# Projecting the next pass's queries, keys and values during the later stages of a two-layer decoder

## Time and profile before

| | |
|---|---|
| Median of 3 runs | 1396.28 us (1387.24 to 1396.66) |
| Profiled execution | 1388.13 us, span 1386.4 us |
| Granted TensorE clock, mean | 0.963 |
| PE busy | 1161.0 us, 84% |
| DVE, ACT, POOL busy | 54%, 53%, 27% |
| DMA | 14 GB/s over the span |

### The profile page before, as it was taken

How to read it: one execution, slowest core, us unless ns; L and a number is a source line. 1 busy time by engine, 2 the same in 40 slices (tenths; PEclk the granted TensorE clock), 3 DMA queues, 4 the chain that set the end, 5 groups by cost and what they waited for, 6 DMA issues and landing times.

```text
span 1386.4 us, 19831 instructions
## 1 busy us (share of the span) xinstructions
PE 1161.0 (84%) x6458; PEld 770.1 (56%) x6458; DVE 750.3 (54%) x1815; ACT 732.8 (53%) x1866; POOL 380.4 (27%) x881
## 2 busy tenths in 40 slices
PE   6897876999899976799889977699989997779955
PEld 2454544775555644676455554477555564467643
DVE  1563375655464368546545437655545436855644
ACT  1555345575465355557456534556645635555833
POOL 1232301542034310153213430154203332016420
PEclk9998998999999999899999999899999999989978
DMA  9101300000000000000000000000000000000000
GB/s 248 63 1 54 93 1 1 1 1 1 1 0 17 1 23 1 3 0 1 1 1 16 1 23 1 2 1 1 1 1 0 17 1 1 1 1 1 1 0 16
DMA packets 27895, 20.77 MB, mean 15 GB/s; under 512 B 14412, under 2 KB 27148, under 8 KB 27660
## 3 DMA queue, kind: packets, MB, share of 16 engines
q1 hardware_dynamic: 27196, 17.83, 5.0%
q10 hardware_dynamic: 592, 1.59, 0.3%
HBM read 17.32 MB, written 2.10 MB: 14 GB/s over the span
## 4 chain that ended last, share of the span: by engine, by line
PE 64%; DVE 15%; ACT 10%; issue 7%; POOL 3%; DMA 1%; ACTq 0%; SPq 0%; POOLq 0%; DVEq 0%
PE PS L495 8%; PE PS L559 7%; PE PS L841 7%; PE PS L482 5%; PE PS L572 5%; PE PS L547 4%; PE PS L586 4%; PE PS L617 4%; PE PS L602 4%; PE PS L815 3%; PE PS L706 2%; PE PS L692 2%; PE PS L853 2%; ACT work L1316 1%; DVE work L1591 1%
## 5 line engine op out<-in xcount | busy, mean ns | idle before, releaser
L1849 POOL TENSOR_TENSOR rstd<-var,minus_half 128x2 f32<-128x2 f32 x80 | 56.4, 705 | 522.3 <-DVE nmean L1409 522.3
L1138 ACT ACTIVATE work<-PS,nmax 128x256 f32<-128x256 f32 x256 | 117.9, 472 | 99.5 <-DVE nmax L1461 99.5
L1844 POOL TENSOR_TENSOR pool_pause<-minus_half 128x1 f32<-128x1 f32 x96 | 18.6, 194 | 440.3 <-DVE inv L1468 359.0
L1316 ACT ACTIVATE work<-PS,nmax 120x256 f32<-120x256 f32 x256 | 118.4, 483 | 24.7 <-DVE nmax L1726 24.5
L841 PE MATMUL PS<-work 128*120 128x256 f32 x512 | 119.7, 384 | 3.9 <-ACT work L1101 3.9
L1461 DVE TENSOR_REDUCE nmax<-PS 128x2 f32<-128x512 f32 x128 | 82.2, 684 | 68.7 <-PE PS L572 68.2
L1863 POOL TENSOR_SCALAR work<-work,inv 128x256 f32<-128x256 f32 x256 | 118.1, 483 | 0.0
L1726 DVE TENSOR_REDUCE nmax<-PS 120x2 f32<-120x512 f32 x128 | 86.3, 686 | 53.3 <-PE PS L841 48.6
L841 PEld LDWEIGHTS PS<-work 128*120 128x120 f32 x512 | 90.8, 183 | 29.8 <-issue 12.8
L1903 POOL TENSOR_SCALAR work<-work,head_mask 128x120 f32<-128x120 f32 x256 | 107.3, 447 | 0.0
L1109 ACT ACTIVATE x_room<-res,nshift,rstd 128x256 f32<-128x256 f32 x96 | 52.3, 592 | 101.9 <-POOL nshift L1851 101.9
(11 more groups left out here) (258 smaller groups left out, 2439.9 us busy)
## 6 DMA issues: line engine op xcount, KB each, us to landing
xa<-in_x_dram SPq DMA_DIRECT2D x4, 512.0 KB, 3.7
out_dram<-x_room SPq DMA_DIRECT2D x4, 512.0 KB, 3.7
rows<-in_rows_dram ACTq DMA_DIRECT2D x1, 1536.0 KB, 8.5
late<-in_L_attn_W_dram SPq DMA_DIRECT2D x2, 768.0 KB, 7.6
wv<-in_L_attn_kernel_dram SPq DMA_DIRECT2D x2, 512.0 KB, 8.9
wq<-in_L_attn_kernel_dram SPq DMA_DIRECT2D x2, 512.0 KB, 9.5
wk<-in_L_attn_kernel_dram SPq DMA_DIRECT2D x2, 512.0 KB, 7.7
wo<-in_L_attn_WO_dram SPq DMA_DIRECT2D x2, 512.0 KB, 7.7
```

Source lines behind the costliest of these rows:

```text
L1138: op = act.activation(e0[:, u % 2, st, hh, :], bank(2 + hh)[:, st * S:(st + 1) * S], ACT.Exp, bias=nmax0[:, u % 2, hh, st:st + 1], accum_o ...
L1316: op = act.activation(e1[:, par, r, kv, :], bank(4 + n % 4)[0:M, kv * S:(kv + 1) * S], ACT.Exp, bias=nmax1[:, par, r, kv:kv + 1], accum_ou ...
```

## The change

All 24 projections of a pass (8 half value tiles, 8 query tiles, 8 key tiles) are made before its attention begins. For pass 0 they stand at the start (`project_first`). For passes 1 to 3 they are spread over the pass before:

- `turn_input` at units 10 and 11 of the self-attention loop, from a second load of x into its own place (`x_t`, `load_x_to_turn`), copied by DVE (`keep_input`).
- In the cross-attention of layer 0 the eight value projections: two ahead of the first turn of the normed x, two behind the first query projection, four in the loop, each ahead of a weighing.
- In the feed-forward queries 0 to 3 (0 ahead of the turns of the quantized x, 1 to 3 in the tile loop), at the head of layer 1 queries 4 to 7.
- At the end of layer 1's cross-attention keys 0 to 5; in coupling rounds 0 and 1 keys 6 and 7.

Their copies out of PSUM: values and queries on ACT, keys on ACT (even) and DVE (odd). Each copy stands in its engine's queue at a fixed place, shown below. q0 and k0 now hold all eight head pairs, o0t lies over q0 (so the output projection waits for its own copies only and q0 is overwritten as it is used up), the scratch areas are laid out anew, and the PSUM banks of all later stages are moved so that bank 7, and at times 5 and 6, are free for the projections; `weigh_x` has one bank where it had two, the quantized turns one where they had two.

In attention the scores run one unit ahead, in banks 0/1 and 2/3 in turns: `scores0(u+1)` and `max0(u+1)` in the place of u. The loops over passes are written out (`for` in place of `Fori`) on all engines, SP's queue loads x and the context one pass earlier, and the DMA scratch size is set to 2048. In the attention loop nothing else on DVE or POOL changes its order.

The diff, cut to its core (the first part is PSUM and layout, then SP, PE, ACT, DVE):

```diff
+        SCORE_X = (2, 0)
+        TOKEN_X = (3, 6)
+        ATTEND = (4, 5, 3, 6)
+        SCORE_1 = (3, 4, 5, 6)
+        MLP_OUT = (2, 1)
+        QUERY_1 = (2, 0)
+        HIDDEN = (2, 6)
+        VALUE_FILL = (7, 6, 7, 6, 7, 7, 7, 7)
+        QUERY_FILL = (7, 7, 7, 7, 7, 5, 7, 5)
+        KEY_FILL = (7, 5, 7, 5, 7, 5, 7, 5)
...
-        turned_x = view(x3_room, 0, P, [KD, N])
-        work = sb("work", [P, 14016])
-        q0 = view(work, 12288, P, [2, N])
-        k0 = sb("k0", [P, 2, NB, S])
+        x_t = view(x3_room, 0, P, [T, D])
+        turned_x = sb("turned_x", [P, KD, N])
+        V, Q, K, E, R = 0, 4096, 8192, 12288, 16384
+        work = sb("work", [P, R + 2240])
+        v0 = view(work, V, P, [T, H * DH0])
+        q0 = view(work, Q, P, [J, N])
+        k0 = view(work, K, P, [J, NB, S])
+        e0 = view(work, E, P, [2, TS, 2, S])
+        e0t = view(work, E + 2048, P, [2, 2, TS, S])
-        o0t = view(work, 8192, P, [J, N])
+        o0t = q0
...
+        def load_x_to_turn(sp, it):
+            if not first_pass(it):
+                sp.wait_ge(turned["xa"].sem, turned["xa"].at(it - 1, NB))
+            if not (isinstance(it, int) and it < 2):
+                sp.wait_ge(o1_kept.sem, o1_kept.at(it - 2, GX))
+            sp.dma_start(x_t[:, :, :], x[it * NB:(it + 1) * NB].rearrange("b (t p) d -> p (b t) d", p=P)).then_inc(xt_in.sem, 16)
...
+            load_x_to_turn(sp, 1)
+            load_ctx(sp, 1)
...
+            load_x(sp, 1)
+            for it in range(1, NI - 1):
+                load_x_to_turn(sp, it + 1)
                 store(sp, it - 1)
+                load_ctx(sp, it + 1)
+                load_x(sp, it + 1)
...
+            def values0(it, n):
+                t, h = n // 2, n % 2
+                if n == 0:
+                    pe.wait_ge(kept["xa"].sem, kept["xa"].at(it, NB))
+                elif n > 1:
+                    pe.wait_ge(v0_kept.sem, v0_kept.at(it, n - 1 if n < 5 else n))
...
+            def queries0(it, j):
+                if j == 0:
+                    pe.wait_ge(v0_kept.sem, v0_kept.at(it, 2 * T))
+                elif j == 5:
+                    pe.wait_ge(silu_done.sem, silu_done.at(it - 1, T))
+                else:
+                    pe.wait_ge(q0_kept.sem, q0_kept.at(it, j if j < 5 else j - 1))
+                for k in range(KD):
+                    mm = pe.matmul(bank(QUERY_FILL[j]), wq0[:, k, j * P:(j + 1) * P], turned_x[:, k, :],
+                                   start=(k == 0), stop=(k == KD - 1))
+                mm.then_inc(q0_done.sem, 1)
...
+            def keys0(it, j):
+                if j == 0:
+                    pe.wait_ge(q0_kept.sem, q0_kept.at(it, J))
+                elif j == 1:
+                    pe.wait_ge(p1_done.sem, p1_done.at(it - 1, GX * HC))
+                else:
+                    read = (k0_kept_a, k0_kept_v)[j % 2]
+                    pe.wait_ge(read.sem, read.at(it, j // 2))
...
+            def scores0(it, u, last=None):
                 j, b = u // NB, u % NB
-                pe.wait_ge(q0_kept.sem, q0_kept.at(it, j + 1))
-                pe.wait_ge(k0_kept.sem, k0_kept.at(it, j + 1))
-                if u > 0:
-                    pe.wait_ge(p0_done.sem, p0_done.at(it, 2 * u))
+                if u == 0:
+                    pe.wait_ge(q0_kept.sem, q0_kept.at(it, J))
+                    pe.wait_ge(k0_kept_a.sem, k0_kept_a.at(it, J // 2))
+                    pe.wait_ge(k0_kept_v.sem, k0_kept_v.at(it, J // 2))
+                elif u == 1:
+                    if last is not None:
+                        pe.wait_ge(tf_tanh.sem, tf_tanh.at(last, CB))
+                else:
+                    pe.wait_ge(p0_done.sem, p0_done.at(it, 2 * (u - 1)))
-                        mm = pe.matmul(bank(2 + hh)[:, st * S:(st + 1) * S],
-                                       q0[rows, j % 2, b * S + st * P:b * S + (st + 1) * P],
-                                       k0[rows, j % 2, b, :], start=True, stop=True)
+                        mm = pe.matmul(bank(2 * (u % 2) + hh)[:, st * S:(st + 1) * S],
+                                       q0[rows, j, b * S + st * P:b * S + (st + 1) * P],
+                                       k0[rows, j, b, :], start=True, stop=True)
...
-                    pe.wait_ge(q0_kept.sem, q0_kept.at(it, J))
-                    pe.wait_ge(k0_kept.sem, k0_kept.at(it, J))
+                    pe.wait_ge(p0_done.sem, p0_done.at(it, 2 * (U0 - 1)))
...
+            def weigh_x(it, m, then=None):
                 b, c = m // KD, m % KD
                 pe.wait_ge(tx_kept.sem, tx_kept.at(it, 2 * m + 2))
                 if m == 0:
                     pe.wait_ge(vx_kept.sem, vx_kept.at(it, 1))
-                if m > 1:
-                    pe.wait_ge(ox_kept.sem, ox_kept.at(it, m - 1))
+                    if then is not None:
+                        pe.wait_ge(v0_kept.sem, v0_kept.at(then, 4))
+                else:
+                    pe.wait_ge(ox_kept.sem, ox_kept.at(it, m))
...
                 if then is not None:
-                    scores0(then, 0)
+                    if r < CYCLES - 1:
+                        keys0(then, J - 2 + r)
+                    else:
+                        scores0(then, 0)
...
+            def turn_input(it, b):
+                if b == 0:
+                    pe.wait_ge(xt_in.sem, xt_in.at(it, 16))
+                    if not first_pass(it):
+                        pe.wait_ge(vx_kept.sem, vx_kept.at(it - 1, 1))
+                else:
+                    pe.wait_ge(kept["xa"].sem, kept["xa"].at(it, b))
+                turn(it, "xa", x_t, b, 7)
+            def attn0(it, last=None, then=None):
                 for u in range(U0 + 2):
-                    if 0 < u < U0:
-                        scores0(it, u)
-                    if u // 2 + 1 < J:
-                        project0(it, u // 2 + 1, u % 2)
+                    if u + 1 < U0:
+                        scores0(it, u + 1, last)
...
+                    if then is not None and u in (10, 11):
+                        turn_input(then, u - 10)
...
+            def cross0(it, then=None):
+                if then is not None:
+                    for n in range(2):
+                        values0(then, n)
...
                 queries_x(it, 0)
+                if then is not None:
+                    for n in range(2, 4):
+                        values0(then, n)
                 turn_normed(it, "x1", xs["1"], 1)
                 for n in range(UX + 1):
...
+                    if then is not None and n in (1, 3, 5, 7):
+                        values0(then, 4 + n // 2)
                     if n >= 3 and n % 2 == 1:
-                        weigh_x(it, (n - 3) // 2)
+                        weigh_x(it, (n - 3) // 2, then)
...
+            def ffn0(it, then=None):
+                if then is not None:
+                    queries0(then, 0)
                 turn_quantized(it, 0)
...
+                    if then is not None and 1 <= t < T:
+                        queries0(then, t)
                     if 3 <= t:
                         down(it, t - 3)
                 down(it, T - 2)
                 turn_hidden(it, T - 1)
...
+            def attn1(it, then=None):
+                if then is not None:
+                    for j in range(4, 7):
+                        queries0(then, j)
                 turn_normed(it, "h", xs["h"], 0)
                 gates(it, 0)
                 values_m(it, 0)
+                if then is not None:
+                    queries0(then, 7)
                 turn_normed(it, "h", xs["h"], 1)
                 outputs_m(it, 0)
                 gates(it, 1)
-                values_m(it, 1)
+                values_m(it, 1, then)
...
                 turn_normed(it, "z0", xs["z0"], 0)
                 weigh_1(it, 2 * GX - 1)
                 out_1(it, 0)
+                if then is not None:
+                    keys0(then, 0)
                 turn_back(it, 1)
                 if then is not None:
-                    turn_input(then)
-                    pe.wait_ge(p1_done.sem, p1_done.at(it, GX * HC))
-                    values0(then, range(0, T // 2))
+                    for j in range(1, 3):
+                        keys0(then, j)
...
+                    for j in range(3, J - 2):
+                        keys0(then, j)
...
+            project_first()
             scores0(0, 0)
...
-            with pe.Fori(1, NI) as it:
-                layer1(it - 1, then=it)
-                layer0(it, last=it - 1)
-            layer1(NI - 1)
+            one_pass(0, then=1)
+            for it in range(1, NI - 1):
+                one_pass(it, last=it - 1, then=it + 1)
+            one_pass(NI - 1, last=NI - 2)
...
                 apply_norm(it, "1", of_res, xs["1"], 0)
+                if then is not None:
+                    for n in range(2):
+                        keep_v0(then, n)
                 keep(it, "x1", 0)
...
+                    if then is not None and n in (1, 3, 5, 7):
```

(29 more changed lines are left out.)

528 lines of the change are left out of this document (277 added, 251 removed).

## The result

The changed kernel takes 1453.87 us (median of four, 1451.99 to 1455.32), the kernel before 1392.03 in the same comparison: ratio 1.0444, interval [1.0395, 1.0493], so slower by 62 us. The forecast was 1432, range 1378 to 1458: the sign and the range held, the size was 22 us short.

A forecast was written before the change was run, and what follows sets the result against it. PE was taken to bound self-attention, with chains of waits bounding the other stages. Terms 24 - 9 - 42.9 + 68.6 = +40.7 us on the profiled 1388.13 gave 1429, plus 3 for the median: 1432 us, range 1378 to 1458.

The forecast's parts named there:

- Reading of the bound: PE bounds self-attention; in the other stages its idle time lies inside chains of waits, so added projections lengthen them.
- Rival (a): Stages outside attention: the moved projections land in idle PE time and cost nothing; whole 1354 us; chance 0.18.
- Step 1: Attention loop, passes 1 to 3: without projections a unit falls from 5.02 to 3.55 us; net -42.9 us.
- The circle: Attention's loop of turn, DVE copy, inverse, POOL normalization and next turn sets the unit at 3.55 us.
- what is given back: Attention: sums, norms, context units and input turns that hid beside PE now show, about 6.6 us per pass.
- Step 2: First pass: all 24 projections precede the first score, +24 us; its attention loop gains, -9 us.
- Steps 3 and 4: Passes 0 to 2: value projections lengthen cross-attention's chain, +11.75 us per pass; ACT's norms wait behind query copies, +9.6.
- the sign that I named: Changed profile: ACT idle 4 us or more before apply_norm 2(0) and 3(0), released by PE projections; otherwise step 4 is wrong.
- Step 5: Per pass: tail with six projections instead of ten, -2 us; coupling with two key projections put in, +3.5.
- Rival (c): PE's granted clock: fills shorten low-clock stretches, at most 9 us per pass, so 1405; no chance of its own.

The follow-up runs named there:

- experiment 2: Changed kernel with VectorE's reciprocal of unit u's sums in self-attention taken before the copy of unit u-1's turned weights: 1407.17 us, ratio 1.0106.
- Experiment 1: Changed kernel with ScalarE's norms queued ahead of the copies of query tiles 0 and 4, tiles 5 and 6 copied behind h's first norm: 1420.42 us, ratio 1.0203.
- Experiment 5: Changed kernel plus two projections' worth of unneeded matmuls (3.6 us) behind the last key projection, ahead of the coupling: 1444.62 us, ratio 1.0356.
- experiment 8: Kernel before with its loops over passes written out on all engines, nothing else changed: 1388.91 us, ratio 0.9976.
- experiment 4: Changed kernel with the projections for passes 1 to 3 and their copies cut to one column, waits and queue places kept: 1380.31 us, ratio 0.9911.
- experiment 7: Changed kernel with experiment 6's reorderings and eight projections per pass moved to where TensorE was seen idle: 1353.65 us, ratio 0.9712.
- Experiment 9: Experiment 7's kernel plus unneeded matmuls around the coupling in passes 0 to 2 and the last pass: 1339.24 us, ratio 0.9623.
- experiment 6: Changed kernel with the ScalarE and VectorE reorderings of experiments 1 and 2 together: 1375.21 us, ratio 0.9864.
- experiment 3: Changed kernel with five key projections at the end of layer 1's cross-attention done twice, 9 us of unneeded PE work: 1478.41 us, ratio 1.0612.

## Why the prediction was right, and where it was short

The 26.5 us that the sum is short on the spans are 16.3 in the coupling of passes 0 to 2, 7.1 in attention, 1.1 ahead of the first score, 2.6 in the last pass and 2.4 from h to z0, less 3.1 in the tail and from x1 to h.

- **Reading of the bound: right.** PE's idle time outside attention was mostly not free *where the projections were put*. Rival (a), 0.18, needed under 9.2 us per pass exposed (9.3 by its own terms); the stages outside attention showed 28 (21.1 from x1 to h with the two tiles ahead of it, 0.8 from h to z0, -2.8 in the tail, 8.9 in the coupling).
- **Step 1, attention: mechanism right, size 7 us short over four passes.** The circle gives 3.62 us per plain unit (3.55 forecast), and experiment 2 confirms it. The term that was mis-sized is what is given back: the two context units take 2.2 more than a plain one, not 0.8 (5.83 against 3.62).
- **Step 2, first pass: right** for the projections (+25.1 against +24); the attention in it won 6.5 (with value tiles 0 and 1 taken out) and not 9.
- **Steps 3 and 4: right.** +52.9 against +53.6. Each loop projection shows 1.7 (9.16 against 7.4; forecast 1.75). Experiment 1 shows what the ACT position is worth over three passes: 24.5 from x1 to h, forecast 28.8, and 7.9 more from h to z0 (from h to x4 46.9 us per pass against 48.5 to 50.2), where I had looked for nothing. Of the sign that I named, ACT idle of 4 us or more ahead of both norms, one is there in full (8.25) and one in part (2.86).
- **Step 5, tail and coupling: the step that failed.** Tail -8.4 (forecast -6). For the coupling I priced only the two projections, 3.5 per pass; they show about that (the 1.98 and 1.88 us pieces). But the coupling grew by 8.9. In pass 1, 4.1 of it is clock: 2.56 in the first round's matmuls, 1.57 in the third's; over passes 0 to 2 the three rounds' matmuls are 13 longer. Another 3.9 of this kind is in the last pass, whose instructions are the same in both kernels (30.3 us of PE busy before, 34.3 after). Experiment 5 shows the cause for the first round, 7 us in three passes. The third round is slow in the kernel before as well once its loops are written out (experiment 8): against that profile the coupling grew by 20.0, not 26.8, and some 12 of this is the two projections. For the last pass the cause is open: its first round took 4.55 in the kernel before, 4.61 in experiment 4 and about 6.2 in the changed kernel and its other variants up to experiment 7, with the same 8.4 us idle ahead of c0. Experiment 9, which filled several gaps of the last pass at once, has 44.7 us there in place of 50.1.
- **Rival (c), the clock, had the wrong sign.** I read the earlier trace rows as a stretch that fills would shorten, and forgot that ten projections that kept PE busy up to c0 were being cut to six. The Trainium skill ("TensorE: Matmul & The Clock Gate", "HAM oscillation — how this bites in real kernels") warns of gaps in PE's work; experiment 5 agrees with it (6.18 to 3.62 us with the gap filled), and it spoke against this change as much as for it.
- **Rival (a) was half a truth.** The Trainium skill ("Perfetto Trace Analysis", "Optimization Strategy") says that interleaving regimes of different bounds may gain; it does here once the queue positions are mended: experiment 6 gives 0.9864, experiment 7 0.9712. I was right that this change does not reach it.
- **A misread row.** I had the copies on engines under 70% busy in all these stages. For ACT that holds (61% at most), for DVE it does not: the earlier trace rows has it at 71% in the cross-attention and 81% in the feed-forward. Of the projections' copies for passes 1 to 3 only the odd key tiles are on DVE, in the tail and the coupling, where it is at 56% and less, so the sum doesn't change. Yet a copy on DVE held up the chain in the tail of experiment 3: the place of a copy in the queue counts, not the engine's share.
- **Not split:** the rest of the coupling's growth (about 1 us per pass with the start of attention in it), and why the second round changed sides between kernels whose coupling is the same (5.41 in one, 3.84 in experiment 2), as the third did between the kernel before and experiment 8.

## What to carry to other kernels

Idle time of an engine is a place in its queue, not a sum: work put behind the instruction that waits costs its full time (1.7 of 1.78 us per value tile), in front of it less, from next to nothing (the feed-forward of experiment 1) to most of its time where another wait of the same chain takes over (1.3 of 1.98 in experiment 7). When work of the next iteration is woven in, look first at its *copies* on the other engines: an in-order queue makes everything behind a copy wait for the matmul it copies, and here that was worth more (33 us) than the matmuls' placement (22). And when an engine stops being the bound, look for the circle of waits that takes its place: one reciprocal moved ahead of a copy was worth 47. And when work is taken away from in front of a stage on TensorE, price that stage at the lower clock as well.

## What the runs showed of the hardware

- TensorE doing useless work made the kernel faster: 3.6 us of it in each of passes 0 to 2 took 9.3 off the whole (experiment 5), and in experiment 9, with more of it, some 14 us came off.
- The spread of the kernel before goes with its granted clock, from run to run: 1386.7 us at 0.966, 1392.2 at 0.961, 1396.6 at 0.956.
- The same sixteen matmuls of the coupling's first round, passes 0 to 2, took 3.62 us in every profile with 0.64 to 1.01 us idle ahead of c0 (the kernel before, experiments 5, 8 and 9), and 4.55 to 6.18 in those with a gap of 3.6 to 5.2. Among these the length of the gap doesn't fix the value: 4.07 us idle went with 6.18, 4.08 with 4.58 in experiment 2, 5.16 with 4.81 in experiment 4.
